# Constant operands of VectorE's per-step operations placed in PSUM: a two-layer graph network on one core

## The reference, cut to what matters

```
def _rgcn_layer(x, src, dst, edge_type, w_rel, root, bias):      # twice
    seg = dst * 10 + edge_type
    sums = segment_sum(x[src], seg);  cnt = segment_sum(1, seg)
    mean = (sums / max(cnt, 1)).reshape(N, 10, -1)
    return einsum('nrd,rdo->no', mean, w_rel) + x @ root + bias

def _L1_gnn_ref(x, edge_index, W_l, W_r, att, bias):             # H = 4 heads of C = 32
    xj, xi = (x @ W_l)[src], (x @ W_r)[dst]
    e = leaky_relu(xi + xj, 0.2)
    score = einsum('ehc,hc->eh', e, att)
    ex = exp(score - segment_max(score, dst)[dst])
    alpha = ex / (segment_sum(ex, dst)[dst] + 1e-16)
    return segment_sum(alpha[..., None] * xj, dst) + bias
```

## Time and profile before

| what | value |
|---|---|
| time, median of 3 runs | 15228.2 us (15210.8 to 15228.5) |
| the profiled execution | 15226.5 us, span 15224.9 us |
| POOL busy | 10366.4 us (68%) |
| PE busy | 6961.8 us (46%) |
| DVE busy | 6411.4 us (42%) |
| ACT busy | 3901.9 us (26%) |
| passes p1, p2 | 871 to 4961 us, 5255 to 9193 us |
| score pass | 9450 to 13692 us |
| attend | 13907 to 15162 us |

### The profile page before, as it was taken

One profiled execution on the slowest core, in us unless ns is written; L12 is line 12 of the kernel. 1 busy time (PEld: TensorE's weight loads), 2 busy tenths in 40 slices (PEclk: granted clock), 3 DMA queues, 4 the chain that ended last, 5 costly groups with the idle time before them and its releaser, 6 DMA issues. The chain is left out here.

```text
span 15224.9 us, 188787 instructions
## 1 busy us (share of the span) xinstructions
PE 6961.8 (46%) x31334; PEld 5984.5 (39%) x31335; DVE 6411.4 (42%) x10363; ACT 3901.9 (26%) x12831; POOL 10366.4 (68%) x10305
## 2 busy tenths in 40 slices
PE   5334444444444744444444445444444444444776
PEld 2123333333333333333333334333333333334775
DVE  4742222222222311111111114666666666668777
ACT  3222222222222322222222222111111111112554
POOL 0057777777777377777777773777777777773665
PEclk9655555555555855555555555555555555557998
DMA  7411111111111511111111112555545555542555
GB/s 244 130 36 50 50 50 50 50 50 50 50 50 50 199 52 52 52 52 52 52 52 52 52 52 67 144 145 145 145 145 145 145 145 145 146 142 86 164 164 163
DMA packets 683155, 1471.13 MB, mean 97 GB/s; under 512 B 193660, under 2 KB 259705, under 8 KB 676489
## 3 DMA queue, kind: packets, MB, share of 16 engines
q0 software_dynamic: 331360, 749.89, 18.2%
q1 hardware_dynamic: 324838, 707.28, 14.3%
q10 hardware_dynamic: 26918, 13.52, 0.4%
HBM read 1117.41 MB, written 352.52 MB: 97 GB/s over the span
## 5 line engine op out<-in xcount | busy, mean ns | idle before, releaser
L838 POOL DMA_INDIRECT p_g<-ytab,p_i x6250 | 6123.0, 980 | 2222.5 <-issue 1707.5
L816 PE MATMUL p_pg<-p_v,p_oh 128*128 x14480 | 3440.9, 424 | 4624.3 <-ACT p_v L876 3468.9
L816 PEld LDWEIGHTS p_pg<-p_v,p_oh 128*128 128x128 f32 x14480 | 3077.9, 319 | 4987.7 <-issue 4987.7
L838 POOL DMA_INDIRECT a_g<-xltab,a_i x3125 | 3289.1, 1053 | 962.5 <-issue 952.0
L791 DVE TENSOR_TENSOR A<-p_pg,A 128x128 f32 x1448 | 422.3, 292 | 6098.4 <-PE p_pg L816 6000.0
L1011 PE MATMUL a_pg<-A,a_oh 128*128 x7240 | 1754.5, 431 | 2515.7 <-DVE a_oh L957 2515.7
L1011 PEld LDWEIGHTS a_pg<-A,a_oh 128*128 128x128 f32 x7240 | 1577.5, 327 | 2692.7 <-issue 2692.3
L876 ACT ACTIVATE p_v<-p_g,wgt_all 128x128 f32<-128x128 f32 x6250 | 1960.4, 388 | 469.0 <-issue 440.3
L870 ACT ACTIVATE p_i<-rel_all 128x5 int32 (+1 forms) x1250 | 260.1, 208 | 5346.9 <-DMA p_g<-ytab,p_i 5346.9
L1216 POOL TENSOR_TENSOR s_v<-s_x,scores 128x512 f32<-128x512 f32 x625 | 792.9, 1282 | 663.0 <-PE s_pg L816 408.9
L777 DVE TENSOR_TENSOR p_oh<-cols,local 128x640 f32<-128x640 f32 x1456 | 1196.9, 822 | 37.7 <-PEq L556 12.7
(11 more groups left out here) (181 smaller groups left out, 3411.9 us busy)
## 6 DMA issues: line engine op xcount, KB each, us to landing
a_dst<-in_dst_dram SPq DMA_DIRECT2D x625, 320.0 KB, 3.7
xj_dram<-a_g SPq DMA_DIRECT2D x625, 320.0 KB, 2.2
s_x<-xj_dram SPq DMA_DIRECT2D x625, 320.0 KB, 3.1
p_g<-ytab,p_i POOLq DMA_INDIRECT x6250, 2.5
ytab<-steps POOLq DMA_DIRECT2D x98, 640.0 KB, 6.7
ytab<-t_y POOLq DMA_DIRECT2D x98, 640.0 KB, 3.2
ea<-in_edge_attr_dram SPq DMA_DIRECT2D x50, 1176.0 KB
a_g<-xltab,a_i POOLq DMA_INDIRECT x3125, 3.0
```

Of the source, the lines that this page charges most:

```text
L816: last = t.matmul(pg[k][:, 0:width], onehot[k][:, q * P:(q + 1) * P], V[:, ds(at + q * width, width)], start=(q == 0), stop=(q == G - 1))
L838: pool.indirect_dma_start(gbuf[k][:, q * D:(q + 1) * D], None, rows, bass.IndirectOffsetOnAxis(ap=stage[k][:, q:q + 1], axis=0)).then_inc( ...
```

## The change

The operands of VectorE's per-step operations that stay the same over a whole stage are read from PSUM in place of SBUF: the column numbers in `sum_engines` (`cols` becomes `colsp`), and in the score pass the node numbers (`node`) and the attention vector (`attb` becomes `attp`). Each is filled once per stage by VectorE: a copy of 128 values with a wait in the two passes and in `attend`, and in the score pass the same tensor_scalar as before with its result now in PSUM, plus a copy of 128 values. `colsp` and `attp` have a bank of their own, `node` has two. L977 and L991 are not touched, nor are L772, L791 and L970; no instruction of another engine differs.

```diff
-        def sum_engines(block, name, onehot, pg, V, width, s_v, s_pe, also=None, localise=False):
+        def sum_engines(block, name, onehot, colsp, pg, V, width, s_v, s_pe, also=None, localise=False):
+            s_cp = sem(f"{name}_cols_set")
...
                     v.tensor_tensor(onehot[k][:, :].rearrange("p (t n) -> p t n", t=G),
-                                    cols[:, :].rearrange("p (a n) -> p a n", a=1).to_broadcast([P, G, P]),
+                                    colsp[:, 0:P].rearrange("p (a n) -> p a n", a=1).to_broadcast([P, G, P]),
                                     here.rearrange("p (t a) -> p t a", a=1).to_broadcast([P, G, P]),
                                     ALU.is_equal).then_inc(s_oh, 1)
...
+                v.tensor_copy(colsp[:, 0:P], cols[:, :]).then_inc(s_cp, 1)
+                dve.wait_ge(s_cp, 1)
                 for s in range(AHEAD):
                     match(s, s, True)
...
+                colsp = psum(st, f"{name}_cols", [P, 512])
...
-                node = sbuf(st, "node", [P, SCOLS * P])
+                node = psum(st, "node", [P, 2 * 512])
+                attp = psum(st, "attp", [P, 512])
...
-                        v.tensor_scalar(node[:, :], base[:, :], rowid[:, 0:1], None, ALU.add).then_inc(s_add, 1)
+                        v.tensor_scalar(node[:, 0:SCOLS * P], base[:, :], rowid[:, 0:1], None, ALU.add)
+                        v.tensor_copy(attp[:, 0:D], attb[:, :]).then_inc(s_add, 1)
                         dve.wait_ge(s_add, 1)
...
-                                    v.tensor_tensor(lk, lk, attb[:, :].rearrange("p (a d) -> p a d", a=1).to_broadcast([P, G, D]),
+                                    v.tensor_tensor(lk, lk, attp[:, 0:D].rearrange("p (a d) -> p a d", a=1).to_broadcast([P, G, D]),
                                                     ALU.mult).then_inc(s_wt, 1)
...
+                colsp = psum(st, "s_cols", [P, 512])
```

More of the change, by code:

```diff
@@ L856, in rgcn_pass @@
                     gather_engine(block, ytab.rearrange("n (r d) -> (n r) d", d=D), stage, gbuf, s_stage, s_g, s_v)
-                    sum_engines(block, name, onehot, pg, V, D, s_v, s_pe, localise=first)
+                    sum_engines(block, name, onehot, colsp, pg, V, D, s_v, s_pe, localise=first)
                     @block.scalar
@@ L1161, in attend @@
                 with nc.Block() as block:
-                    sum_engines(block, "s", onehot, pg, V, W, s_v, s_pe, s_va)
+                    sum_engines(block, "s", onehot, colsp, pg, V, W, s_v, s_pe, s_va)
                     @block.scalar
```

## The result

The changed kernel takes 14694.9 us (median of 4 runs, 14686.5 to 14699.3) against 15228.0 us for the kernel before: a ratio of 0.9652, 95% interval 0.9635 to 0.9669, or 3.5% faster. The profiled execution has a span of 14691.1 us against 15224.9, 534 us less. The forecast was 14690.

A forecast was written before the change was run, and what follows sets the result against it. GpSimd's gather stream, lengthened by VectorE operations with two SBUF inputs, was taken to bound three stages, and VectorE's loop body attend; 188 + 35 + 181 + 132 = 536 us less gave 14690 us, range 14625 to 14790.

The forecast's parts named there:

- The floor of the gathering stages: In p1, p2 and score pass, GpSimd's own stream of 3125 gathers with their issue sets a floor of 3903 us.
- p1 and p2, 188 and 35 us: In the two passes, the match loses its second SBUF input and stops lengthening gathers: 188 and 35 us less.
- Score pass, 181 us: In the score pass, L957 and L982 stop holding gathers: 100 + 81 = 181 us less.
- L977's share: In the score pass, L977 still reads Z twice from SBUF; its 161 us stay, range 110 to 230 us.
- Attend, 132 us: In attend, shorter first and second matches take a loop body from 6.90 to 6.17 us: 132 us less.
- TensorE as the next in line: Rival in attend: TensorE's body binds, bodies 6.5 to 6.8 us, 60 to 119 us less gain, 14750 to 14809; chance 8%.
- An operation with a PSUM operand costs no more: For VectorE's changed operations, no difference in duration was taken, from 0.83 us against 0.82 and 0.83 without PSUM.
- a slow repeated read: Rival for VectorE's changed operations: a repeated operand reads slowly from PSUM; 15659 us at 2.5 times the duration; chance 2%.
- the operand's place: Rival in the score pass: a second input in PSUM frees nothing, so no gain there, 14871 us; chance 6%.
- The rule that would have limited the gain to attend: Rival: gathers are held by something coinciding with the match, so only attend gains, 15094 us; chance 2%.
- Filling the constants cost nothing: Four copies of 128 values, under 1 us each, run beside other work and cost nothing; uncovered 4 us.

The follow-up runs named there:

- the control of that chip: Kernel before with awaited values clamped at zero and only the first two matches of an attend body reading PSUM, score pass as before; score pass 5157 us.
- the controls: Kernel before and changed kernel, each with every awaited value first clamped at zero: 15189.7 us and 14686.4 us.
- x_k01: Kernel before with clamped awaited values, only the first two of four matches in an attend body reading PSUM: attend 1147 us against 1258 with all in SBUF.
- x_k23: Kernel before with clamped awaited values, only the last two of four matches in an attend body reading PSUM: attend 1256 us against 1258 with all in SBUF.
- x_passes: Kernel before with clamped awaited values, only the matches of p1 and p2 reading PSUM: 14977.9 us against 15189.7 with all in SBUF.

## Why the prediction was right, point by point

- **The floor of the gathering stages.** 3125 times 1.249 us, 3903 us by the prediction, was met at 3900 in both passes. POOL's busy time was forecast near 2950 and is 2948.
- **p1 and p2, 188 and 35 us.** 190 and 38. The longest gather of the passes was forecast not to exceed 0.96 us. Ten of 6,250 do, six of them with 0.961; the other four, up to 1.015, are the first two of each pass. What lengthens those was not looked for.
- **Score pass, 181 us.** 176. The split by operation was confirmed by busy times only: 70 and 79 us where the control of that chip had 85 and 71 by the sorting. L977's share was kept at 161 on the argument that all phases against the gathers are about equally likely; sorting the gathers after the change gives 165. This was the least certain term. In the controls, whose clamps alone shift the phases, it was 130 and 136, so some 30 us of scatter must be allowed for it: that the total came within 5 us of the forecast is in part luck, while the range of 110 to 230 for this term holds them all.
- **Attend, 132 us.** 133, by the mechanism given: only the first two matches of a body count, x_k01 against x_k23. (The working took 1247.7 us for 723 steps, but 723 starts span 722: a body was 6.91 us before, which makes 134.) TensorE as the next in line was right in kind, but its rival's bodies of 6.5 to 6.8 us were too long. It added the register load to the products in full, while the bodies of 5.85 to 5.96 us in the traces show the two overlapped in part. The prediction kept 6.17 us because such bodies existed, and that was the sounder argument: 0.2 to 0.3 us of room were left, and the clamps of the controls, which lengthen TensorE's body to 6.31, were enough to use them up.
- **An operation with a PSUM operand costs no more.** In the passes the match has a median of 823 ns, 824 before; in x_k01 it takes 814 at least with PSUM and 806 without. The medians of the other two fell from 826 to 820 (L963) and from 818 to 811 (L988). The rivals of a slow repeated read and of the operand's place are refuted. The Trainium skill's page "VectorE: DVE Perf Modes", section on the trn2 errata, puts 62 more cycles on a PSUM source than on one in SBUF, some 65 ns by the prediction's estimate; for these operations, with one input in PSUM and one in SBUF, the differences are -7 to 8 ns.
- **The rule that would have limited the gain to attend.** The Trainium skill's page "SBUF — State Buffer", section "Who interferes with whom", infers that a tensor_tensor does not hold up the making of descriptors. x_passes took 217 us from two stages in which GpSimd does nothing but issue gathers. What is held seems to be the read of row numbers that an indirect gather makes some 0.14 us after its start; that it is this read, and not another, is argued from times and was not tested by itself.
- **Filling the constants cost nothing** that can be seen: p1, p2, score pass and attend sum to the difference of the spans within 3 us.

## What to carry to other kernels

Look in the timeline for GpSimd instructions that are lengthened by just what is left of a VectorE operation (the gathers here end 0.8 us behind it, whatever their start); if that operation has two inputs in SBUF and one of them is a constant, a free PSUM bank for the constant releases GpSimd at no price in VectorE's time. Count the gain only where GpSimd's stream or the delayed operation is what the stage waits for: half of attend's shortened matches were worth nothing, and on the slower chips, where TensorE held up the passes, they showed no such gain. Moving an operand that TensorE has to write again is another matter, since the longer hold of the buffer can cost more than the free way to SBUF gave.

## What the runs showed of the hardware

- An indirect gather of 128 rows on GpSimd takes 0.94 us with 0.305 us between two, and a VectorE operation with two SBUF inputs lengthened single ones to 1.60 us. It did so only where it was running 0.14 us after the gather's start. In the score pass before, all 359 gathers that met the product with the attention vector so were lengthened, and none of the 361 that met the sum with one input in PSUM.
- A register load by VectorE takes 2.95 us for 13 words and 0.30 for one; TensorE's takes 1.58 for 15. Over the stretches read here the long ones stay within 3% of that, whatever the engines have to do. Products already queued run on beside it.
- The same kernel takes 15.2 ms on some chips and 17.3 to 17.5 on others. On those the gathered rows land as soon as elsewhere, but TensorE's stream falls behind again and again with no wait in the profile: over a hundred stretches of some 10 us in p1 of x_k23, none in x_b. I had not expected that. Its cause is open.
